# Splitting the experts' second factor and its weighted activations into high and low parts: three reduced-format passes in place of one full 32-bit product

## What is computed

```python
base_out = jnp.einsum('btd,od->bto', x, base_W) + base_b
logits = jnp.einsum('btd,nd->btn', x, router_W) + router_b
probs = jax.nn.softmax(logits, axis=-1)
topk_p, topk_i = jax.lax.top_k(probs, E)
...
h = jnp.einsum('btd,erd->bter', x, A)
lora = jnp.einsum('bter,eor->bto', h * w[..., None], B) * SCALING
return base_out + lora
```

## Time and profile before

| what | value |
|---|---|
| median of 3 runs | 1011.15 us (1010.93 to 1012.07) |
| the profiled execution, its own time | 1008.72 us |
| its span | 1006.9 us |
| PE busy | 991.5 us, 98% of the span |
| DVE, ACT, POOL busy | 47%, 41%, 34% |
| PE's share of the chain that ended last | 94% |

### The profile page before, as it was taken

One profiled execution on the slowest core, in us unless ns is written; L12 is line 12 of the kernel. 1 busy time (PEld: TensorE's weight loads), 2 busy tenths in 40 slices (PEclk: granted clock), 3 DMA queues, 4 the chain that ended last, 5 costly groups with the idle time before them and its releaser, 6 DMA issues.

```text
span 1006.9 us, 14845 instructions
## 1 busy us (share of the span) xinstructions
PE 991.5 (98%) x5168; PEld 840.5 (83%) x5168; DVE 472.8 (47%) x956; ACT 413.6 (41%) x1110; POOL 337.8 (34%) x317
## 2 busy tenths in 40 slices
PE   7999999999999999999999999999999999999998
PEld 5888888888888888888888888888888887888886
DVE  4674712462155305532364235622472287666664
ACT  6554333432453244334442354234423354555640
POOL 3351314113330424041414051314131424587640
PEclk9999999999999999999999999999999999999999
DMA  8022011102110201010101010101101103210002
GB/s 311 21 85 55 26 59 61 35 12 72 42 52 0 83 24 59 10 62 21 62 31 62 21 62 31 48 35 62 31 21 63 42 1 107 113 33 2 1 1 84
DMA packets 16402, 50.52 MB, mean 50 GB/s; under 512 B 3056, under 2 KB 3312, under 8 KB 15600
## 3 DMA queue, kind: packets, MB, share of 16 engines
q1 hardware_dynamic: 15360, 48.75, 14.2%
q10 hardware_dynamic: 1008, 1.32, 0.4%
HBM read 47.97 MB, written 2.10 MB: 50 GB/s over the span
## 4 chain that ended last, share of the span: by engine, by line
PE 94%; DVE 2%; issue 1%; POOL 1%; ACT 1%; DMA 1%; SPq 0%; ACTq 0%; DVEq 0%
PE bank L1282 34%; PE bank L1340 17%; PE bank L1294 17%; PE bank L1401 9%; PE bank L1324 6%; PE bank L1304 6%; PE bank L1315 3%; PE bank L1394 2%; PE bank L1478 1%; PE bank L1498 1%; PE bank L1541 1%; DMA craw<-in_ctx 1%; POOL wvo L361 1%; DVE xt L878 0%; DVE rinv L918 0%
## 5 line engine op out<-in xcount | busy, mean ns | idle before, releaser
L1282 PE MATMUL bank<-xt,wq 128*128 128x512 f32 x768 | 186.4, 393 | 0.0
L1282 PE MATMUL bank<-ct,wk 128*128 128x512 f32 x768 | 181.6, 392 | 1.3 <-DVE ct L844 1.3
L1340 PE MATMUL bank<-wvo,ao 128*128 128x512 f32 x768 | 180.6, 392 | 0.0
L1294 PE MATMUL bank<-wvo,ct 128*128 128x512 f32 x768 | 178.0, 390 | 0.2 <-POOL wvo L361 0.2
L1294 PEld LDWEIGHTS bank<-wvo,ct 128*128 128x128 f32 x768 | 143.5, 188 | 29.8 <-POOL wvo L361 0.6
L1282 PEld LDWEIGHTS bank<-ct,wk 128*128 128x128 f32 x768 | 142.7, 188 | 30.5 <-DVE ct L844 1.9
L1282 PEld LDWEIGHTS bank<-xt,wq 128*128 128x128 f32 x768 | 142.4, 188 | 29.1
L1340 PEld LDWEIGHTS bank<-wvo,ao 128*128 128x128 f32 x768 | 142.4, 188 | 28.6
L361 POOL TENSOR_TENSOR wk<-stage,wk 128x512 fp32r<-128x512 f32 x32 | 42.3, 1321 | 296.9 <-ACT wk L542 296.9
L361 POOL TENSOR_TENSOR wvo<-stage,wvo 128x512 fp32r<-128x512 f32 x64 | 81.8, 1305 | 162.3 <-ACT wvo L542 162.3
L558 ACT ACTIVATE prob<-prob,nmax 128x128 f32<-128x128 f32 x256 | 99.3, 390 | 59.9 <-DVE nmax L909 59.9
(11 more groups left out here) (145 smaller groups left out, 1117.6 us busy)
## 6 DMA issues: line engine op xcount, KB each, us to landing
stage<-in_w SPq DMA_DIRECT2D x63, 512.0 KB, 3.3
xraw<-in_x SPq DMA_DIRECT2D x2, 1024.0 KB, 11.9
bias<-in_bias SPq DMA_DIRECT2D x8, 256.0 KB, 2.6
cs<-in_ctx SPq DMA_DIRECT2D x1, 2048.0 KB, 7.6
out<-acc SPq DMA_DIRECT2D x8, 256.0 KB, 2.2
craw<-in_ctx ACTq DMA_DIRECT2D x4, 256.0 KB, 5.8
craw<-in_ctx SPq DMA_DIRECT2D x4, 256.0 KB, 6.4
stage<-in_w_key SPq DMA_DIRECT2D x1, 1024.0 KB, 4.7
```

Of the source, the lines that this page charges most:

```text
L1282: mm = pe.matmul(bank[un_of[first][u] % RING][:, :], w[:, i, c, :], t[:, j, c, half(s)], start=(c == 0 and i + j == 0), stop=(c == KC - 1 ...
L1294: mm = pe.matmul(bank[un_of[first][u] % RING][:, :], ct[:, i, c, b * P:(b + 1) * P], wvo[:, j, c, :], start=(c == 0 and i + j == 0), stop= ...
L1340: mm = pe.matmul(bank[to][:, :], ao[:, h, i, b * P:(b + 1) * P], wvo[:, j, h, :], start=(h == heads[0] and i + j == 0), stop=(h == heads[- ...
```

## The change

Two tiles are laid over the dead key weights: `pwr`, high and low parts of the turned, weighted activations (8 KB of a partition), and `wbr`, high and low parts of the experts' factor (4 KB). ACT makes the high part of the factor once (`experts_hi`), POOL the low part. ACT's `weighted_out` now writes the high part of the activations and a new DVE instruction (`weighted_lo`) subtracts it from the bank to give the low part. PE's `experts(u)` makes three passes in place of one full 32-bit matmul, and waits for the low parts.

```diff
+    pwr = nc.alloc_sbuf_tensor_at("pwr", [P, 2, B, ER], fp32r, offset=small0)
+    wbr = nc.alloc_sbuf_tensor_at("wbr", [P, 2, D], fp32r, offset=small0 + 8192)
...
+                pool.wait_ge(S["bm_hi"], 1)
+                pool.tensor_tensor(wbr[:, 1, :], wbm, wbr[:, 0, :].bitcast(fp32), ALU.subtract).then_inc(S["bm_lo"], 1)
                 for u in range(4, B):
                     add_row(u - 1, R_BASE, "xn2", "rsb")
                     norm(u, 2)
...
                 def weighted_out(q):
 
                     act.wait_ge(S["hw_T"], q + 1)
-                    act.activation(ptw[:, part(q), :], bank[4 + q][:, :].rearrange("p (u e) -> p u e", u=HB),
+                    act.activation(pwr[:, 0, part(q), :], bank[4 + q][:, :].rearrange("p (u e) -> p u e", u=HB),
                                    ACT.Copy).then_inc(S["hw_out"], 1)
+
+                def experts_hi():
+
+                    act.wait_ge(s_bm1, 16)
+                    act.wait_ge(S["k_mm"], B)
+                    act.activation(wbr[:, 0, :], wbm, ACT.Copy).then_inc(S["bm_hi"], 1)
...
                         split_hi("base", u - 1)
                         split_hi("ra", u - 1)
+                experts_hi()
                 hi(1, 2)
                 normed(3, 2)
...
+                def weighted_lo(q):
+
+                    dve.wait_ge(S["hw_out"], q + 1)
+                    dve.tensor_tensor(pwr[:, 1, part(q), :], bank[4 + q][:, :].rearrange("p (u e) -> p u e", u=HB),
+                                      pwr[:, 0, part(q), :].bitcast(fp32), ALU.subtract).then_inc(S["hw_lo"], 1)
...
                 lo(6, 2)
                 lo(7, 2)
+                weighted_lo(0)
                 x4(0)
                 x4(1)
...
                 adapters(1)
+                weighted_lo(1)
                 for u in HALVES[1]:
                     x4(u)
...
                 def experts(u):
 
-                    pe.wait_ge(S["hw_out"], u // HB + 1)
+                    pe.wait_ge(S["hw_lo"], u // HB + 1)
                     if u == 0:
-                        pe.wait_ge(s_bm1, 16)
-                    pe.matmul(bank[base_bank[u % HB]][:, :], ptw[:, u, :], wbm, start=False, stop=True).then_inc(S["o_mm2"], 1)
+                        pe.wait_ge(S["bm_lo"], 1)
+                    for i, j in PASSES:
+                        mm = pe.matmul(bank[base_bank[u % HB]][:, :], pwr[:, i, u, :], wbr[:, j, :], start=False, stop=(i == 1))
+                    mm.then_inc(S["o_mm2"], 1)
```

More of the change, by code:

```diff
@@ L244, in build @@
                  "q_rr", "q_T", "q_out", "s_mm", "s_max", "s_neg", "s_exp", "s_rc", "s_rg", "p_T", "p_out", "pv", "x3",
-                 "ra", "ra_out", "router", "lg_exp", "top", "hw", "hw_T", "hw_out", "o_mm", "o_mm2", "x4",
+                 "ra", "ra_out", "router", "lg_exp", "top", "hw", "hw_T", "hw_out", "hw_lo", "bm_hi", "bm_lo", "o_mm", "o_mm2", "x4",
                  "rows", "rsf", "rsb", "cs"]
```

## The result

| what | before | changed |
|---|---|---|
| median, 20 runs each | 1010.17 us (1008.08 to 1012.07) | 1008.96 us (1006.54 to 1009.72) |
| ratio | | 0.9984, interval 0.9977 to 0.9991 |
| profiled execution, its span | 1008.72, 1006.9 us | 1009.45, 1007.6 us |

The change makes the kernel faster by 0.16%, 0.9 to 2.3 us by the interval. A second series (12 runs of the changed kernel, 29 of the one before) gave 0.9988 (0.9979 to 0.9998). The forecast that the difference stays within 0.2% holds. The time does not: 1008.96 us lies 0.14 us under the range, and the gain by the medians, 1.2 us, is larger than the 0.9 us that I had forecast. One run of the kernel before, in a later series of ten, took 1691.06 us at a mean granted clock of 0.558 and is left out of the median of that series.

The account below looks back on a forecast made before the run. TensorE, busy 98% of the span, was taken to bound the kernel. Product -1.38, first hand-over +0.28 and stores +0.2 gave -0.9 us, from 1011.15 to 1010.25 us; range 1009.1 to 1012.0 us, within 0.2% at 0.88.

Parts of the forecast that it names:

- The level: Whole kernel: the forecast 0.9 us gain was taken from 1011.15 us, the runs' median, 2.4 us above the profiled 1008.72 us.
- so the clock is no part of this case: TensorE over the whole span: granted clock at nine tenths or more in every slice, the higher level, 2.4 GHz.
- all covered: Last stage, rival: wake-up hidden and stores keep up, -1.33 us, 1009.8 us; chance 0.14.
- Part 1: Experts' products on PE: three split passes, 0.687 us, replace 0.86 us per batch, saving 1.38 us over eight.
- rule of four equal passes: Experts' products: the skill's true FP32 takes four passes, so three would save an estimated 1.72 us; not followed.
- Part 2: Hand-over before the first half of products: DVE's new low part makes PE stall 0.28 us, between 0.05 and 0.5.
- Part 3: Hand-over before the second half of products: low part ready with 1.4 us of cover, costs nothing.
- Part 4: Factor's high part on ACT, low part on POOL: norm(4) some 0.45 us later, absorbed before norm(7), cost nothing.
- Part 5: Tail, last stores: at 0.83 us each they cannot all follow the quicker pace; cost taken as 0.2 us.
- The tail gives it back: Tail, rival: hand-over costs 0.5 us and stores land at 3.1 us, +0.2 us, 1011.4 us; chance 0.13.
- POOL's rival: POOL's low part reaches norm(7), lengthening PE's wait before adapters(6): +0.4 us, 1011.55 us; chance 0.06.
- open weight loads: Experts' products, rival: 8 more weight loads each cost 0.190 us in the open, +0.6 us, 1011.75 us; chance 0.03.

Follow-up runs that it names:

- the two that take the wait away: Changed kernel without DVE's low part of the activations, 22.05 us from first turning to end; changed kernel with first half's hand-over in two pieces, 22.0 us.
- all three edits: Changed kernel with POOL's wait, DVE's low part of batch 6 early and first hand-over in two pieces: 1003.62 us, 0.9941 of before.

## Why the prediction was right or wrong

**The level (the number that failed).** "The median of the runs is 2.4 us above it; the same 0.9 us from 1011.15" took the shown median as the kernel's level, and all cases and the range were added to it. Twenty runs have it at 1010.17 us, 0.98 us lower. The forecast of 1010.25 us was 1.29 us too high: 0.98 of it is this step, 0.31 the difference (0.9 forecast, 1.21 by the medians). The same range moved down by 0.98 us would reach from 1008.1 to 1011.0 us and hold the 1008.96. The 2.4 us gap between profile and runs was the sign, since the part outside the span is 1.8 us and already in the 1008.72 us. The sentence "so the clock is no part of this case" rested on that one profiled execution, which has no fall of the clock; of the runs of this kernel with a clock on record 23 of 38 have a mean of 0.998, and the fall costs 1.6 us. Whether the three runs of 1010.93 us and more had it is not on record, and 1.6 us would not be the whole of the gap. A small slip beside it: "all covered, less 0.6" is 1009.2 us, not 1009.1. That the difference stayed within 0.2% was right, but narrowly: the interval goes to 0.23%.

**Part 1, right.** A pass took 0.229 us: twelve in 2.75 us where nothing waits. Eight batches save 1.38 us of PE. The estimate by the rule of four equal passes, 1.72 us, is too high; in this kernel the full form costs 3.75 passes.

**Part 2, right, a little high.** Predicted 0.28 us of stall; 0.23 us by the run with the full product, 0.25 us by the two that take the wait away. The reckoning was right in kind: in the changed kernel the low part was ready at 987.16 us, 0.08 us ahead of the 987.24 at which PE's chain stood, and still the twelve passes took 3.00 us in place of 2.75.

**Part 3, right.** The second stretch began without a wait. The changed kernel's low part ran from 999.51 for 0.69 us, ready 1.4 us ahead of 1001.61.

**Part 4, right in its result.** No new wait of PE. norm(4) came 0.5 us later, as reckoned, and the idle time before norm(7) shrank from 1.53 to 1.19 us. But the reason was incomplete: the nearest danger was not norm(7). It was the turning of the last probabilities, with 0.87 us to spare.

**Part 5, the term that was mis-sized.** I took 0.2 us for stores that cannot follow at 0.69 us. They can: the last one landed 2.0 us after its issue, as before, and even at 0.66 us in 2.1. The mean of 315 GB/s that I divided by held gaps between stores; it was a rate of issue, not a limit. The row that I read gave the share beside it: 315 GB/s at 0.85 is 371 GB/s at a full share, 0.71 us for a store and not 0.83, and 371 GB/s is what the changed kernel moved. With this term at nothing and the stall at 0.25 us the sum is -1.13 us, near the 1.2 us that the trace has; the last 0.1 us are partly base's 0.05 us.

**The rivals.** The one closest to what happened is "all covered", though not by its reasons: the wake-up was not hidden. "The tail gives it back" and the open weight loads fall: 24 loads of 188 ns lie within passes of 0.229 us. POOL's rival needed over 0.87 us more of delay.

## What to carry to other kernels

A full 32-bit matmul of this form is worth 3.75 passes of the split form, so splitting one gains a fifth of its time on TensorE and needs an engine step more in front of it; hand over in pieces where that step is on the path. When a profiled execution lies off the median of the runs by more than the part outside its span, look for a place at which executions differ before forecasting a level, and take the level from many runs. Where PE idles in a kernel that is 98% PE, ask which engine ran beside the one it waited for: a wait put on the bystander was worth more here than the change.

## What was not expected of the hardware

- PE idle for 2.3 us, after some 780 us without a wait, was followed in some executions by a granted clock of 0.5 to 0.6 for about four us (1.6 us lost), in others not at all: 19 of 29 runs with a mean of 0.998, one with 0.999 and 9 with 1.000, same kernel, same chip. With the idle time gone it came in none of 16, nor in the 5 of the kernel with all three edits. The shorter waits of 0.66 and 1.06 us were not followed by it in the two traces. What decides between the two outcomes was not found.
- POOL's 128x512 subtractions made DVE's instruction on 128x4 numbers last 1.27 us in place of 0.16. The reciprocal next to it, with one input, took 0.16 us beside POOL and 0.17 us without.
- One execution ran with TensorE at a quarter of its pace throughout, at a recorded clock of 1.00 (POOL's and DVE's instructions kept their durations). Its cause stays open.

One correction to the text ahead of the prediction: `wt_a` takes 16 KB of a partition, not 32; the two new tiles take 12 of them.
